# Normalised product of a 0/1 matrix with float32 weights: per-tile waits, an 18-tile ring and pieces of 4 down to 1 tiles, in place of units of 4 tiles in 4 slots

## The reference

```python
entities = jnp.einsum('be,le->bl', entity_idxs, W)   # x: 1024 x 12500, W: 128 x 12500
s = jnp.sum(entity_idxs, axis=1)
s_safe = jnp.where(s != 0, s, 1.0)
scale = jnp.where(s != 0, 1.0 / s_safe, 1.0)
y = entities * scale[:, None]                        # 1024 x 128
```

## Time and profile before

| | |
|---|---|
| median of 3 runs | 151.04 us (150.97 to 151.16) |
| the profiled execution | 151.15 us, span of its instructions 149.4 us |
| PE, PEld busy | 135.2 us (91%), 76.4 us (51%) |
| DVE, ACT busy | 94.5 us (63%), 84.1 us (56%) |
| HBM read | 57.60 MB, 389 GB/s over the span |
| mean granted TensorE clock | 0.996 |

### The profile page before, as it was taken

One profiled execution on the slowest core, in us unless ns is written; L12 is line 12 of the kernel. 1 busy time (PEld: TensorE's weight loads), 2 busy tenths in 40 slices (PEclk: granted clock), 3 DMA queues, 4 the chain that ended last, 5 costly groups with the idle time before them and its releaser, 6 DMA issues.

```text
span 149.4 us, 2230 instructions
## 1 busy us (share of the span) xinstructions
PE 135.2 (91%) x785; PEld 76.4 (51%) x785; DVE 94.5 (63%) x110; ACT 84.1 (56%) x129; POOL 0.7 (0%) x13
## 2 busy tenths in 40 slices
PE   0597998799999999999999999999999999999960
PEld 0244654455555555555555655655555555665530
DVE  0471953746756845955954954864864778965593
ACT  3571852735735834844843854763763677955173
POOL 1000000000000000000000000000000000000000
PEclk9999999999999999999999999999999999999998
DMA  5999999999999999999999999999999999999022
GB/s 147 404 427 459 405 454 399 449 420 425 444 410 449 410 444 420 434 434 410 454 415 434 420 439 429 410 459 410 434 425 439 408 425 416 414 406 342 16 70 75
DMA packets 5719, 58.19 MB, mean 390 GB/s; under 512 B 638, under 2 KB 1534, under 8 KB 2514
## 3 DMA queue, kind: packets, MB, share of 16 engines
q1 hardware_dynamic: 5714, 58.13, 92.6%
HBM read 57.60 MB, written 0.52 MB: 389 GB/s over the span
## 4 chain that ended last, share of the span: by engine, by line
DMA 56%; PE 35%; DVE 4%; SPq 1%; issue 1%
DMA xw<-main 56%; PE acc L417 35%; DVE y_sum L366 2%; DVE low_max L320 1%; SPq L167 1%; DVE row_sum L363 0%; SPq L163 0%; SPq L165 0%; DVE row_sum L357 0%; DVE row_sum L360 0%; DVE any_low L396 0%; PE acc L470 0%; DVE inexact L398 0%
## 5 line engine op out<-in xcount | busy, mean ns | idle before, releaser
L417 PE MATMUL acc<-parts_main,xw 128*128 128x385 bf16 x640 | 108.2, 327 | 3.8 <-DMA xw<-main 3.0
L417 PEld LDWEIGHTS acc<-parts_main,xw 128*128 128x128 bf16 x640 | 61.3, 98 | 50.7 <-issue 8.4
L320 DVE TENSOR_REDUCE low_max<-xw 128x2048 uint16 x20 | 45.5, 2278 | 0.0
L243 ACT ACTIVATE parts_main<-xw 128x512 bf16<-128x512 bf16 x20 | 12.7, 635 | 47.0 <-DMA xw<-main 37.7
L309 DVE TENSOR_TENSOR w_rest<-xw 128x512 f32<-128x512 f32 x20 | 13.8, 692 | 40.0 <-DMA xw<-main 40.0
L250 ACT ACTIVATE act_out<-xw 128x2048 bf16<-128x2048 uint16 x20 | 37.9, 1893 | 0.0
L316 DVE TENSOR_TENSOR parts_main<-w_rest 128x512 bf16<-128x512 f32 x21 | 14.6, 695 | 0.7
L246 ACT ACTIVATE parts_main<-w_rest 128x512 bf16<-128x512 bf16 x21 | 13.3, 635 | 2.0
L417 PE MATMUL acc<-parts_short,xw_short 84*128 84x385 bf16 x8 | 2.7, 522 | 5.5 <-ACT parts_short L246 5.5
L320 DVE TENSOR_REDUCE low_max<-xw_taper 128x1 f32<-128x1024 uint16 (+1 forms) x6 | 6.1, 1038 | 1.4 <-DMA xw_taper<-ends 1.3
L250 ACT ACTIVATE act_out<-xw_taper 128x1024 bf16<-128x1024 uint16 (+1 forms) x6 | 5.4, 906 | 1.7 <-DMA xw_taper<-ends 1.6
(11 more groups left out here) (50 smaller groups left out, 38.2 us busy)
## 6 DMA issues: line engine op xcount, KB each, us to landing
xw<-main SPq DMA_DIRECT2D x20, 2304.0 KB, 16.3
xw_taper<-ends SPq DMA_DIRECT2D x2, 1024.0 KB, 24.9
x_final<-ends SPq DMA_DIRECT2D x3, 512.0 KB, 27.8
xw_taper<-ends SPq DMA_DIRECT2D x1, 1408.0 KB, 21.8
xw_ramp<-ends SPq DMA_DIRECT2D x1, 1280.0 KB, 7.5
xw_taper<-ends SPq DMA_DIRECT2D x1, 1280.0 KB, 18.8
xw_taper<-ends SPq DMA_DIRECT2D x2, 512.0 KB, 27.1
xw_ramp<-ends SPq DMA_DIRECT2D x1, 704.0 KB, 4.9
```

Of the source, the lines that this page charges most:

```text
L243: nc.scalar.activation(parts[0:rows, 0:n, 0:L], top(words, n), ACT.Copy)
L320: nc.vector.tensor_reduce(low_max[0:rows, bass.ds(col, 1)], low(words, n), AX.XY, ALU.max).then_inc(dve_checked, 1)
L417: return nc.tensor.matmul(acc[:, b, 0:N], x, parts, start=first, stop=last)
```

## The change

The tiles are dealt out anew. A **head** (one tile of x, with the W of 7 tiles: its own, the first unit's, and that of 3 of the last 6 tiles) is issued first by SP, and the short tile at the same time by ACT, ahead of all its other work. The next 90 tiles go through a ring of 18 tiles, in 33 pieces of 3, 3, 4 ... 2 ... 1 tiles, with W of the next unit beside each x. A unit is now 3 tiles. TensorE waits for each tile of a unit; GpSimd turns the landing of a piece into a count of tiles (`landed`) on which PE, DVE and ACT wait. The last 6 tiles of x (before: 4) come by banks as `x_final`. In the end part DVE checks a quarter and ACT three quarters of each `x_final` piece, DVE adds the parts of two banks in one instruction, and DVE, not ACT, scales the last bank. The float32 branch is rewritten too; it is not taken.

```diff
+UNIT = 3
+SLOTS = 6
+RING = SLOTS * UNIT
+PIECES = (3, 3, 4, 4, 4,
+          4, 4, 4, 3, 3,
+          4, 4, 4, 3, 3,
+          3, 3, 3, 3, 2, 2, 2,
+          2, 2, 2, 2, 2, 2, 2, 1, 1, 1, 1)
+LAST = 6
+FINAL = ((0, 2, 0, 6), (2, 4, 0, 6), (4, 6, 0, 6), (6, 7, 0, 6), (7, 8, 0, 4), (7, 8, 4, 6))
...
         @block.gpsimd
+            for k, n in enumerate(PIECES):
+                pool.wait_ge(piece_in[k], 16)
+                pool.sem_inc(landed, n)
...
         @block.sync
-            sp.dma_start(xw_short[0:short, :], piece(0)).then_inc(short_in, 16)
...
-            with sp.Fori(1, MAIN // SLOTS) as i:
-                for s in range(SLOTS):
-                    m = SLOTS * i + s
-                    sp.wait_ge(products_done, m - SLOTS + EDGE + 1)
-                    sp.wait_ge(dve_checked, m - SLOTS + EDGE + 1)
-                    sp.wait_ge(act_checked, m - SLOTS + EDGE + 1)
-                    load_main(m, s)
+            sp.dma_start(xw_head[:, :], edge(0)).then_inc(head_in, 16)
+            for k, n in enumerate(PIECES):
+                last_unit = (FIRST_TILE[k] + n - 1) // UNIT
+                if last_unit >= SLOTS:
+                    sp.wait_ge(products_done, used(last_unit - SLOTS))
+                    sp.wait_ge(dve_checked, used(last_unit - SLOTS))
+                    sp.wait_ge(act_checked, used(last_unit - SLOTS))
+                j = FIRST_TILE[k] % RING
+                sp.dma_start(xw[:, j:j + n, :], piece(k)).then_inc(piece_in[k], 16)
...
         @block.scalar
-            act.wait_ge(short_in, 16)
+            act.dma_start(xw_short[0:short, :], edge(1)).then_inc(short_in, 16)
+            act.wait_ge(head_in, 16)
...
+                    act.wait_ge(landed, UNIT * u + UNIT)
+                    act.wait_ge(products_done, used(u + 1 - SLOTS))
+                    split(unit_w(s), parts[:, (s + 1) % SLOTS, :, :], UNIT, (s + 1) % 2, unit_split(u + 1))
...
         @block.vector
-                for b in range(b0, b1):
-                    dve.wait_ge(bank_full, b + 1)
-                    if b == b1 - 1:
-                        row_sum_is_zero(b0, b1, ONES).then_inc(sum_step, 1)
-                    add_parts(b).then_inc(y_summed, 1)
+                dve.wait_ge(bank_full, pair + 1)
+                row_sum_is_zero(b0, b1, ONES).then_inc(sum_step, 1)
+                add_parts(b0, b1).then_inc(y_summed, 1)
...
+            nc.vector.tensor_scalar(y[:, BANKS - 1, :], y_sum[:, BANKS - 1, :], row_sum[:, BANKS - 1, 2:3], None,
+                                    ALU.mult).then_inc(y_last_ready, 1)
...
         @block.tensor
-                    wait_parts(unit_count(m))
-                    pe.wait_ge(main_in[s], 16 * (i + 1))
-                    multiply(main_x(s), T, parts_main[:, s, :, :])
+                    wait_split(unit_split(SLOTS * i + s))
+                    for j in range(UNIT):
+                        pe.wait_ge(landed, RING * i + UNIT * s + j + 1)
+                        mm = multiply(top(unit_x(s))[:, j, :], parts[:, s, j, :])
+                    mm.then_inc(products_done, 1)
```

More of the change, by code:

```diff
@@ L42, in pieces, with rec_kernel, edge, piece @@
         at += rows * cols
-    return table, at
-def rec_kernel(nc, main, ends, out, E):
+    return table
+def rec_kernel(nc, loop, ends, out, E):
     B, L = out.shape
     BANKS = B // P
-    short = E - (TILES + LAST) * P
-    table, _ = pieces(short, B, L)
+    ROW = B + L
+    short = E - (1 + LOOP + LAST) * P
+    table = edges(short, B, L)
     ONES = PARTS * L
     N = ONES + 1
[L53 to L59, removed]
+    NF = len(FINAL)
+    CHECKS = 2 + UNITS + NF
+    FIRST_TILE = [sum(PIECES[:k]) for k in range(len(PIECES))]
+    assert 0 < short <= P and N < 512 and sum(PIECES) == LOOP and SLOTS % 2 == 0
+    assert all(a % RING + n <= RING for a, n in zip(FIRST_TILE, PIECES))
+    def edge(k):
         at, rows, cols = table[k]
         return ends[at:at + rows * cols].rearrange("(p f) -> p f", p=rows)
+    def piece(k):
+        at = FIRST_TILE[k] * P * ROW
+        return loop[at:at + PIECES[k] * P * ROW].rearrange("(p j f) -> p j f", p=P, j=PIECES[k])
     with ExitStack() as ctx:
@@ L190, in load_full @@
[L190 to L233, removed]
@@ L235, in _ @@
+                for k, n in enumerate(PIECES):
+                    for j in range(n):
+                        t = FIRST_TILE[k] + j
+                        sp.wait_ge(full_used, t + 2)
+                        sp.dma_start(kept[:, t % KEPT, 0:ROW], piece(k)[:, j, :]).then_inc(full_in, 16)
+                wait_out()
                 sp.wait_ge(full_ready, BANKS)
@@ new lines, in check, with scale @@
+            def check(k):
+                act.wait_ge(final_in[k], 16)
+                act.wait_ge(act_checked, used(UNITS + k - 2))
+                low_sum(tiles(x_final[k][:, dve_share(k):], 1), 2 + UNITS + k, (k + 1) % 2).then_inc(act_checked, 1)
+            def scale(pair):
+                act.wait_ge(inverse_done, pair + 1)
+                act.wait_ge(y_summed, pair + 1)
+                for b in range(*PAIRS[pair]):
+                    nc.scalar.activation(y[:, b, :], y_sum[:, b, :], ACT.Copy,
+                                         scale=row_sum[:, b, 2:3]).then_inc(y_ready, 1)
@@ L306, in _ @@
+            check(0)
+            check(1)
+            scale(0)
+            check(2)
+            scale(1)
+            check(3)
+            check(4)
+            scale(2)
+            check(5)
+            scale(3)
         @block.vector
@@ new lines, in _ @@
+            lo(parts[:, 0, :, :], UNIT, UNIT_0_REST, UNIT_0_SPLIT)
+            dve.wait_ge(short_in, 16)
+            dve.wait_ge(top_parts_done, HEAD_SPLIT)
+            rest(tiles(xw_short[0:short, B:ROW], 1), 1, SHORT_REST, rows=short)
+            lo(parts_short, 1, SHORT_REST, SHORT_SPLIT, rows=short)
+            rest(tiles(w_alone, ALONE), ALONE, ALONE_REST)
+            lo(parts_alone, ALONE, ALONE_REST, ALONE_SPLIT)
+            dve.wait_ge(ones_set, 1)
+            low_largest(tiles(xw_head[:, 0:B // 2], 1), 0).then_inc(dve_checked, 5)
@@ new lines, in _ @@
+            low_largest(tiles(xw_short[0:short, 0:B // 2], 1), 1, rows=short).then_inc(dve_checked, 1)
+            with dve.Fori(0, ROUNDS) as i:
+                for s in range(SLOTS):
+                    u = SLOTS * i + s
+                    dve.wait_ge(landed, UNIT * u + UNIT)
+                    dve.wait_ge(top_parts_done, unit_split(u - 1))
+                    rest(unit_w(s), UNIT, (s + 1) % 2)
+                    dve.wait_ge(products_done, used(u + 1 - SLOTS))
+                    lo(parts[:, (s + 1) % SLOTS, :, :], UNIT, (s + 1) % 2, unit_split(u + 1))
+                    low_largest(unit_x(s, 0, B // 2), u + 2).then_inc(dve_checked, 1)
@@ L356, in row_sum_is_zero, with check @@
+            def check(k):
+                dve.wait_ge(final_in[k], 16)
+                low_largest(tiles(x_final[k][:, 0:dve_share(k)], 1), 2 + UNITS + k).then_inc(dve_checked, 1)
             def row_sum_is_zero(b0, b1, col):
@@ L417, in product, with multiply, wait_split @@
                 return nc.tensor.matmul(acc[:, b, 0:N], x, parts, start=first, stop=last)
[L419 to L427 removed]
+            def multiply(x, parts, first=False):
+                for b in range(BANKS):
+                    mm = product(b, x[:, b * P:(b + 1) * P], parts, first)
+                return mm
+            def wait_split(count):
                 pe.wait_ge(top_parts_done, count)
@@ L459, in _ @@
-            for k, (b0, b1, j0, j1) in enumerate(FINAL):
-                pe.wait_ge(final_in[k], 16)
-                x = top(x_final[k][:, :], j1 - j0)
+            wait_split(SHORT_SPLIT)
+            multiply(top(tiles(xw_short[0:short, 0:B], 1))[:, 0, :],
+                     parts_short[0:short, 0, :]).then_inc(products_done, 1)
+            with pe.Fori(0, ROUNDS) as i:
+                for s in range(SLOTS):
+                    wait_split(unit_split(SLOTS * i + s))
[3 more added lines that the diff above has]
+                    mm.then_inc(products_done, 1)
@@ L466, in _, with last_parts, last_product @@
                     if j1 == LAST:
+                        yield b, mm
+            def last_parts(j):
+                return parts_alone[:, j, :] if j < ALONE else parts[:, 0, j - ALONE, :]
+            def last_product(b, x, j, c, parts, last):
+                return product(b, top(x)[:, j, c:c + P], parts, last=last)
+            for k in range(NF):
+                pe.wait_ge(final_in[k], 16)
+                for b, mm in last_tiles(k, last_parts, last_product, unit_split(UNITS)):
+                    if b == FINAL[k][1] - 1:
@@ L497, with last_product_full @@
+                def last_product_full(b, x, j, c, w, last):
+                    return product_full(b, x[:, j, c:c + P], w, last=last)
+                for k in range(NF):
+                    for b, mm in last_tiles(k, last_full, last_product_full):
+                        mm.then_inc(full_bank, 1)
```

372 lines of the change are left out of this document (148 added, 224 removed).

## The result

The changed kernel takes 152.0 us (151.93 to 152.18), the one before 151.1 us in the same runs: a ratio of 1.0059 (95% interval 1.0046 to 1.0072). I forecast 148.0 us, in a range of 146.6 to 149.9. The sign was wrong, and the range missed it by 2 us.

A forecast was written before the change was run, and what follows sets the result against it. The data stream was taken to set the pace up to about 120 us, then PE's products. PE's end at 142.7, last scaling at 144.3 and 2.14 for store and exit gave span 146.4, time 148.0 us, range 146.6 to 149.9.

The forecast's parts named there:

- the last term of the sum: After the last scaling at 144.3 us: store and exit take 2.14 us as before, giving a span of 146.4.
- The start: Kernel start: head and short tile both in at 6.8 us, first product at 7.7 instead of 5.55.
- both my bounds, 5.9 and 7.0: Head's landing at the start: 5.9 us if it went first alone, 7.0 by a slower reckoning of the stream.
- The clock: First products on PE: half speed, 0.32 us each, until the clock rises 6.1 us behind the first product.
- The ring and the pieces: Main loop: PE waits at each 4-tile piece, last at 74.1 us, then runs without waits and ends at 142.7.
- Nothing for the wait of each tile: PE's loop: the register instruction and wait for each tile cost zero, with 7.3 us as the bound.
- The rival that carried my chance for slower: PE's loop, second half: each tile's wait costs time, slower overall from 0.06 us per tile, 152.2 at 0.1; chance 0.10.
- The slip of one landing: Data stream: one landing slips by 1.25 us as in the kernel before, and all later ones with it.
- The end part: Behind PE's end: DVE finishes the last banks and the last scaling comes some 1.6 us after PE's end.

The follow-up runs named there:

- run 2: The kernel before, with 64 more float32 products in TensorE's part of the branch that is not taken; 153.83 us, ratio 1.0174.
- run 1: The changed kernel with TensorE's part of the untaken float32 branch cut down to the short tile's 8 products; 149.18 us, ratio 0.9875.
- run 5: The changed kernel, float32 branch whole, with 16 one-column products on TensorE ahead of the wait for the head; 149.23 us, ratio 0.9881.
- run 10: The changed kernel with only 2 one-column products on TensorE ahead of the wait for the head; 149.13 us, ratio 0.9842.
- run 3: The changed kernel with the short tile issued by SyncE right behind the head instead of by ScalarE; 151.85 us, ratio 1.0046.
- run 6: The changed kernel with TensorE's float32 branch body cut and one TensorE wait per unit of 3 tiles instead of per tile; 151.49 us, ratio 1.0017.
- run 4: The changed kernel with the ring in 30 pieces of 3 tiles, without 4s or the final 2s and 1s; 150.56 us, ratio 0.995.
- run 9: The changed kernel with 16 one-column products, short tile on SyncE, and ring pieces of 22 threes, 7 twos and 10 ones; 148.94 us, ratio 0.9841.

## Why the prediction was wrong, step by step

**The step that failed** is the last term of the sum, "With 2.14 for store and exit the span is 146.4". I took the exit over from the kernel before as a constant. It was 5.1 us, 2.95 more, and of this 2.69 is the jump (3,036 against 347 ns). The description of the change says that the float32 branch is rewritten and not taken, and the sum gave it no term. But a branch that is not taken is jumped over, and the change had made TensorE's share of it longer. The row of the jump stood in the trace of before, and no rival asked what it would cost if its target were not there. The Trainium skill has the rule (Runtime: NRT & Kernel Launch, "Instruction fetch mechanics"): a taken branch to a target outside the fetched window has to fetch it before execution goes on. The traces agree: the jump took 3.04 and 3.78 us in the changed kernel and run 2, and 0.23, 0.46 and 0.46 us in runs 1, 5 and 10; I had not looked there. Without the jump the changed kernel is at 149.2, inside the range.

**The start** was right in kind: the first product at 8.5, not 7.7. The head was used from 7.63 instead of 6.8, later than both my bounds, 5.9 and 7.0. I had argued that a second queue brings no more bytes; run 3 shows that it brings fewer in the same time (296 against 413 GB/s from 4 to 5 us): without it the head is used from 5.70, and the stream is 0.55 us earlier. The clock was off too. Before the first product PE was idle, and the first products are 0.32 us apart, the 1.2 GHz level, though the granted clock shown for 8 to 12 us is 1.00. I had let the clock rise 6.1 us behind the first product; it rose after 9.0 us, at 17.48 (weight loads, from the timeline of 8 to 20 us):

```profile
17.16 0.15 PEld L400 LDWEIGHTS acc<-parts,xw 128*128 128x128 bf16 x1 [0.17 <-issue]
17.48 2.57 PEld L400 LDWEIGHTS acc<-parts,xw 128*128 128x128 bf16 x16 [0.17 <-issue]
```

In run 1 it rose after 3.8 us, at 12.30, and PE ends at 143.8 in both, since the waits for landings behind it take in the difference. So this miss cost nothing.

**The ring and the pieces** went as forecast: waits at the 4-tile pieces, the last at tile 44 (75.1, forecast 74.3), then PE at its own pace (0.164 us a product), one wait of 0.16 us at tile 84. I had given that landing 0.4 us to spare at 126.3; it came at about 127.7. Of these 1.4 us 0.9 were there at the landing of 75.0 (0.8 of it from the head), and 0.5 came behind it, where a tile took 1.387 us instead of 1.375 in pieces of 3 and 2 tiles; my sum had such a loss for the 1-tile pieces alone. (The change has six transfers more, 41 against 35, not seven.) PE ended at 143.77, forecast 142.7. Run 6 shows the mechanism, run 4 the worth of the taper.

**Nothing for the wait of each tile** was right: from 75 us to the final tiles PE lost only that 0.16 us and twice under 0.05. The rival that carried my chance for slower did not happen.

**The slip of one landing** came, 1.3 us, at 33.81 (33.81 - 26.97 = 6.84 where 5.50 is the pace):

```profile
26.97 0.56 DVE L297 TENSOR_TENSOR w_rest<-xw 128x384 f32<-128x384 f32 x1 [2.69 <-POOLq L194]
33.81 0.56 DVE L297 TENSOR_TENSOR w_rest<-xw 128x384 f32<-128x384 f32 x1 [4.03 <-POOLq L194]
```

**The end part** took 1.35 us from PE's end to the last scaling, forecast 1.6.

The sum: +1.1 (PE's end), -0.25 (end part), +2.95 (exit) are the 3.8 us by which the span passes 146.4.

## What to carry to other kernels

Compare what lies behind the last useful instruction as closely as what lies before it: ask the trace for the jump of each branch, and treat code that is never run as part of the program whose place and length can cost microseconds. When two versions differ by 1 to 3 us, look first whether the difference is in the work or in the exit; here a gain of 1.9 us stood behind a loss of 2.8. And when PE is only 5% faster than the stream, the last long wait sets the end, however far ahead of it it lies.

## What the runs showed of the hardware

**An instruction fetch delays the data stream.** The slip of 1.25 to 1.35 us in both kernels goes with a q8 fetch. In the changed kernel the queues show it between 28 and 34 us, and none between 22 and 28; in run 5, whose TensorE program is 31 instructions further on (32 more and a wait less), it is the other way round, and the slip moves with it (28.22 - 21.41 = 6.81). The queues of run 5 from 22 to 28 us, and its landings:

```profile
q1 hardware_dynamic: 150, 2.47, 97.0%
q8 instruction: 1, 0.02, 1.1%
```

```profile
21.41 0.56 DVE L297 TENSOR_TENSOR w_rest<-xw 128x384 f32<-128x384 f32 x1 [2.59 <-POOLq L194]
28.22 0.56 DVE L297 TENSOR_TENSOR w_rest<-xw 128x384 f32<-128x384 f32 x1 [4.00 <-POOLq L194]
33.72 0.56 DVE L297 TENSOR_TENSOR w_rest<-xw 128x384 f32<-128x384 f32 x1 [2.69 <-POOLq L194]
```

In run 6 too, with the fetch between 22 and 28 us, a landing due at 26.8 comes at 28.3. With the engines full, one packet of 0.02 MB is never made up for. Its bytes alone would be about 0.04 us of the stream (an estimate: 0.016 MB at 429 GB/s); why it costs 1.3 is not shown. The Trainium skill (Runtime: NRT & Kernel Launch, "Instruction fetch mechanics") calls the crossing of a 16 KiB boundary mostly hidden; here it goes with 1.25 to 1.35 us on all later landings.

**PE's clock can fall inside the stream.** In run 6 PE waits 2.96 us before 28.39. From 29.4 on the products are 0.32 us apart again, the 1.2 GHz level, until 32.6; the granted clock of that stretch is 0.50, and 0.98 in the microsecond ahead of it:

```profile
30.04 0.15 PEld L400 LDWEIGHTS acc<-parts,xw 128*128 128x128 bf16 x1 [0.17 <-issue]
30.37 0.15 PEld L400 LDWEIGHTS acc<-parts,xw 128*128 128x128 bf16 x1 [0.17 <-issue]
```

**Open.** Why run 4, with the same TensorE program as the changed kernel, has its fetch at the end: the place of its instructions in memory is not in the trace. Nor does a count of instructions explain the early fetch: it moved to the stretch from 22 to 28 us both in run 5, with more instructions ahead, and in run 6, with fewer in the loop. Three of the ten executions of run 4 took 149.9 to 150.0 us and seven 150.4 to 150.8. And a single execution of each of runs 9 and 10 was about 1 us shorter than the others (148.04 and 148.13 us); neither was the profiled one.
